# One load for the tiles of two steps in the second phase of a graph-network kernel

## The reference

```python
edge_aggr = jnp.zeros((n, 128)).at[row].add(edge_features)      # 206250 x 128 into 6250 x 128
combined = jnp.concatenate([x, edge_aggr, global_expand], axis=-1) @ W_c + b_c
h = jax.nn.softplus(combined @ W1 + b1)
h = jax.nn.softplus(h @ W2 + b2)
out = _layernorm(x + (h @ W3 + b3), axis=-1)
```

## Time and profile before

| | |
|---|---|
| median of 3 runs | 2045.82 us (2043.21 to 2053.67) |
| the profiled execution's own time | 2045.75 us |
| its span, first to last instruction | 2043.8 us |
| TensorE's granted clock over the span | 0.944 of full |
| busy: TensorE, VectorE, ScalarE, GpSimd | 90%, 64%, 51%, 57% |
| DMA: bytes, mean rate | 413.19 MB, 202 GB/s |
| loads of `members` (L423) | 456 of 258.0 KB, median 3.6 us from issue to landing |

### The profile page before, as it was taken

The page is one execution under the profiler, slowest core; times in us unless marked ns, Lnnn a source line. Parts: engine busy times, 40 slices in busy tenths (PEclk is TensorE's granted clock), DMA queues, the critical chain, the costliest instruction groups (busy, mean ns, idle before and its releaser), DMA issues.

```text
span 2043.8 us, 61008 instructions
## 1 busy us (share of the span) xinstructions
PE 1837.2 (90%) x14853; PEld 1709.6 (84%) x14853; DVE 1309.8 (64%) x3881; ACT 1038.7 (51%) x3479; POOL 1170.9 (57%) x1482
## 2 busy tenths in 40 slices
PE   7888988898898989998998889898988999999986
PEld 4788888888888888887888888788888999999973
DVE  7755555555555555555565555555656998899866
ACT  1443443343444444444443444344446888888886
POOL 1656656656655655665665665565564555555535
PEclk9899988898899999899999898999998999999998
DMA  5488666666656665665565556565657999999942
GB/s 139 156 265 277 198 207 207 202 191 211 207 180 173 174 173 166 175 183 165 172 187 173 172 161 184 163 180 161 186 174 222 299 304 300 296 298 305 304 138 61
DMA packets 166150, 413.19 MB, mean 202 GB/s; under 512 B 28533, under 2 KB 43813, under 8 KB 163896
## 3 DMA queue, kind: packets, MB, share of 16 engines
q1 hardware_dynamic: 103824, 234.69, 38.1%
q0 software_dynamic: 54608, 174.58, 27.5%
q10 hardware_dynamic: 7689, 3.60, 1.0%
HBM read 234.52 MB, written 178.23 MB: 202 GB/s over the span
## 4 chain that ended last, share of the span: by engine, by line
PE 77%; issue 8%; DVE 5%; another core or an unknown queue 3%; POOL 1%; ACT 1%; POOLq 1%; DMA 1%; DVEq 0%; ACTq 0%; SPq 0%
PE ps L1228 51%; PE ps L1300 19%; PE ps L1199 2%; PE ps L1186 2%; DVE arena L803 2%; PE ps L1190 1%; DVE hotc L641 1%; DVE arena L875 1%; PE ps L1335 1%; PE ps L1196 1%; DVE slot_f L660 0%; POOL sums L564 0%; DVE picked L652 0%; POOLq L559 0%
## 5 line engine op out<-in xcount | busy, mean ns | idle before, releaser
L1228 PE MATMUL ps<-arena 128*120 128x129 f32 x9084 | 1229.3, 291 | 98.6 <-issue 87.7
L1228 PEld LDWEIGHTS ps<-arena 128*120 128x120 f32 x9084 | 1141.5, 193 | 130.8 <-issue 117.3
L522 POOL DMA_INDIRECT buckets<-arena,index x757 | 778.8, 1029 | 549.2 <-ACT arena L1013 341.3
L803 DVE TENSOR_SCALAR arena<-slot_no,slot_f 128x360 f32<-128x360 f16 x1514 | 549.1, 415 | 601.3 <-PE ps L1228 332.7
L1013 ACT ACTIVATE arena<-ps 120x387 f32<-120x387 f32 x757 | 372.6, 493 | 851.8 <-PE ps L1228 519.5
L1300 PE MATMUL ps<-mark,members 128*128 128x128 f32 x3648 | 412.7, 276 | 9.0 <-ACT mark L1114 7.1
L1300 PEld LDWEIGHTS ps<-mark,members 128*128 128x128 f32 x3648 | 410.5, 192 | 11.2 <-issue 10.4
L847 DVE TENSOR_SCALAR mark<-node_no,members 128x128 f32<-128x128 f16 x1368 | 360.7, 330 | 55.1 <-DMA members<-buckets 45.9
L564 POOL TENSOR_TENSOR sums<-sums,staged 128x128 f32 x456 | 226.4, 496 | 197.5 <-ACT staged L1102 119.5
L968 ACT ACTIVATE reach<-block_no,arena 128x120 f16<-128x120 f16 x806 | 313.4, 391 | 0.7 <-PE ps L1238 0.7
L1108 ACT ACTIVATE apart<-node_no,members 128x128 f32<-128x128 f16 x456 | 181.0, 397 | 34.3 <-DMA members<-buckets 26.6
(11 more groups left out here) (169 smaller groups left out, 634.6 us busy)
## 6 DMA issues: line engine op xcount, KB each, us to landing
members<-buckets SPq DMA_DIRECT2D x456, 258.0 KB, 3.6
arena<-in_feats SPq DMA_DIRECT2D x201, 516.0 KB
buckets<-arena,index POOLq DMA_INDIRECT x757
xn<-in_x ACTq DMA_DIRECT2D x1, 2800.0 KB
arena<-in_xT SPq DMA_DIRECT2D x11, 250.0 KB, 3.9
out_rows<-xn SPq DMA_DIRECT2D x11, 224.0 KB
buckets<-arena,direct_at POOLq DMA_INDIRECT x98
arena<-in_src SPq DMA_DIRECT2D x1, 805.5 KB
```

Of the source, the lines that this page charges most:

```text
L522: pool.indirect_dma_start(units, bass.IndirectOffsetOnAxis(ap=index[0:SLOTS, s, b:b + 1], axis=0), rows[0:SLOTS, o, :], None).then_inc(sca ...
L803: dve.tensor_scalar(perm[0:TP, b, t, :], slot_no[0:TP, :, :].rearrange("p r b -> p (r b)"), slot_f[0:TP, s, b * TPB + t:b * TPB + t + 1], ...
L1228: mm = pe.matmul(ps[0:SLOTS, MOVED + b, r * ROWF:(r + 1) * ROWF], perm[0:TP, b, t, r * SLOTS:(r + 1) * SLOTS], feat[0:TP, s, b * TPB + t, ...
```

## The change

One load now brings the tiles of two steps, 516 KB, into two neighbouring slots. It is issued when both slots are free, that is, when the later of the two is summed (m + 2 - 8 for m + 1 - 8). It counts one semaphore up for both, so that `members_loaded[m // 2]` stands where `members_loaded[m]` did. In each partition the load has two pieces of 2064 bytes, which lie 258 KB apart in HBM and side by side in SBUF. Lines below the edit stand one lower in the changed kernel.

```diff
--- before.py
+++ after.py
@@ -420,17 +420,18 @@
             sp.wait_ge(filled, 16 * FILLS)
 
             def load_members(s, m):
-                sp.dma_start(members[:, m, :],
-                             buckets[bass.ds(s * TROWS, TROWS), :].rearrange("(p r) f -> p (r f)", r=QR))\
-                  .then_inc(members_loaded[m], 16)
-
-            for m in range(MS):
+
+                sp.dma_start(members[:, m:m + 2, :],
+                             buckets[bass.ds(s * TROWS, 2 * TROWS), :].rearrange("(a p r) f -> p a (r f)", a=2, r=QR))\
+                  .then_inc(members_loaded[m // 2], 16)
+
+            for m in range(0, MS, 2):
                 load_members(m, m)
 
             for c, (t0, nt) in enumerate(chunks):
                 with sp.Fori(1 + c * TURN_X, 1 + (c + 1) * TURN_X if c < NCH - 1 else STEPS // MS) as i:
-                    for m in range(MS):
-                        sp.wait_ge(summed, i * MS + (m + 1 - MS))
+                    for m in range(0, MS, 2):
+                        sp.wait_ge(summed, i * MS + (m + 2 - MS))
                         load_members(i * MS + m, m)
                 sp.dma_start(xt[:, t0 * NP_:(t0 + nt) * NP_], xT[:, t0 * NP_:(t0 + nt) * NP_])\
                   .then_inc(xt_loaded, 16)
@@ -841,7 +842,7 @@
 
 
             def mark_nodes(s, m, turn):
-                dve.wait_ge(members_loaded[m], turn * 16 + 16)
+                dve.wait_ge(members_loaded[m // 2], turn * 16 + 16)
                 wait(dve, summed, s - 3)
                 for r in range(QR - 1):
                     last = dve.tensor_scalar(mark[:, m % 4, r, :], node_no[:, :],
@@ -1103,7 +1104,7 @@
 
 
             def last_apart(s, m, turn):
-                act.wait_ge(members_loaded[m], turn * 16 + 16)
+                act.wait_ge(members_loaded[m // 2], turn * 16 + 16)
                 wait(act, last_marked, s - 1)
                 act.activation(apart[:, m % 2, :], node_no[:, :], ACT.Abs, scale=-1.0,
                                bias=members[:, m, QR * ROWF - 1:QR * ROWF]).then_inc(apart_made, 1)
```

## The result

The changed kernel takes 2133.52 us (median of 4 runs, 2122.50 to 2138.99), the kernel before 2047.76 us (4 runs, 2043.21 to 2053.67): a ratio of 1.0424, with a 95% interval of 1.0392 to 1.0455. The forecast was 2090 us in a range of 2058 to 2125: the direction was right, the loss of 86 us nearly twice the forecast one of 44, and the time lies 8.5 us above the range.

A forecast was written before the change was run, and what follows sets the result against it. TensorE was taken to bound the second phase at 414.6 us, with DMA, VectorE and ScalarE close behind. Pairs at 2.0 us give 456.0, +41.4, plus 0.8 and 2: +44.2 on 2045.75, 2090 us, range 2058 to 2125.

The forecast's parts named there:

- the prediction's ring: Second phase: landing, 0.7 us to step k-1, 1.3 us to next issue, over three pairs; period max(1.80, (L + 2.0) / 3).
- (3): SyncE's issue: the even tile's load goes out one step later, shrinking its room by a step; odd tile unchanged.
- (4): Landing: later for both tiles, since neither counts before 516 KB arrive; 0.8 us for each further tile when the queue is full.
- the room that was left: Second phase before the change: seven steps in the ring, 6.31 us, less 2.0, leave 4.3 us for a load.
- L: Time of a pair's load from issue to landing in the second phase: taken as 4.0 us, between 3.4 and 5.8.
- the sum: Second phase 456.0 us, +41.4; first pair +0.8, xT loads +2; together +44.2 us on 2045.75, giving 2090 us.
- SyncE's halved work: SyncE's loads: half the issues save 0 us, as SyncE waits for TensorE in 370 places.
- The signs that were named: Second phase: landing near 4.0 us, ScalarE's tile waits about 228 and over 100 us, about 456 us, DMA below 0.9, clock 1.00.
- Stays hidden: Rival: pairs land at 3.4 us or sooner, so no change at ScalarE's wait; about 2046 us; chance 0.15.
- the limit of 3.4: Landing in us above which TensorE waits every pair; each 0.1 us of L costs 7.6 us.
- Crowded: Rival: pairs crowd the DMA engines, landing 4.8 us, period 2.27, phase 517 us, 2150 us in all; chance 0.10.
- The third: Rival: waiting every pair lowers TensorE's clock in the second phase, 28 us lost, 2118 us in all; chance 0.08.

The follow-up runs named there:

- run 1: Kernel before with only the issue paired: SyncE waits for the later of two slots, then issues two single 258 KB loads; 1805.66 against 1775.21 us, ratio 1.0171.
- run 2: Kernel before with only the count paired: single loads issued one by one, both tiles wait until both landed; 1795.01 against 1775.21 us, ratio 1.0112.
- run 14: Kernel before with issue and count paired, but two 258 KB loads in a row instead of one of 516 KB; 1839.74 against 1774.30 us, ratio 1.0365.
- run 4: Changed kernel with ScalarE's last_mark(s + 2) put before last_apart(s + 3); 1807.96 us against 1775.21 for the kernel before, ratio 1.0187.
- run 6: Changed kernel with 12 slots for 8, PSUM banks in a ring of six, b3 additions moved; 2076.67 us against 2075.41 for the kernel before, ratio 1.0009.
- run 8: Changed kernel whose loop loads bring only the first half of each piece, 1032 of 2064 bytes; 2072.70 us against 2075.41 for the kernel before, ratio 0.9998.
- run 9: Changed kernel with TensorE's eight passes per step done twice, so that a pair takes 3.6 us; 2472.51 us in one run.
- run 13: The changed kernel unaltered, measured again on one chip beside the two-loads version; 1857.95 us against 1774.30 for the kernel before, ratio 1.0472.
- run 7: Changed kernel with one piece of 4128 bytes per partition instead of two of 2064; 2156.15 us, ratio to the kernel before 1.0384.
- run 5: The changed kernel unaltered, as a yardstick on the other experiments' chip; 2155.46 us against 2075.41 for the kernel before, ratio 1.0388.

## Why the prediction was half right

**The place and the mechanism held.** The loss is in the second phase alone, TensorE waits for tiles, and it does so through ScalarE's look at the first tile of a pair: every stop lies before the odd step, and with ScalarE's order turned before the even one. The table splits the measured periods into the terms of the prediction's ring, (landing + rest) / pairs in the ring. Landings are medians; in run 1 that of the pair's first tile (its row above is for all loads), in run 2 that of its second tile, for which both wait, and in run 14 the time from the first issue to the landing of both. "Rest" is landing to step plus step to issue, the mean over all pairs of the phase:

| kernel | landing | rest | pairs | period by the ring | measured (phase / 228) |
|---|---|---|---|---|---|
| changed kernel | 4.4 | 0.9 + 1.3 | 3 | 2.20 | 500.2 / 228 = 2.19 |
| 1, issue paired | 3.6 | 1.05 + 1.3 | 3 | 1.98 | 452.1 / 228 = 1.98 |
| 2, count paired | 3.4 | 1.05 + 1.3 | 3 | 1.92 | 438.3 / 228 = 1.92 |
| 14, two loads | 4.1 | 0.95 + 1.3 | 3 | 2.12 | 485.6 / 228 = 2.13 |
| 4, mark first | 4.5 | 1.25 + 2.2 | 4 | 1.99 | 451.7 / 228 = 1.98 |
| 6, twelve slots | 4.6 | 2.2, taken over | 5 | 1.36, under TensorE's 1.80 | 413.8 / 228 = 1.81 |

That the sums come out is no proof: the terms are means between the same events, and from one issue to the issue three pairs later they must add up to three periods. The table tells how large each term was. What tests the ring are the periods written down before the runs, with a rest of 2.2 us: 1.93 for run 1 (1.98 measured), 1.93 for run 2 (1.92), 1.91 for run 4 (1.98), and no loss for run 6 (none).

**The later issue and the later landing**, parts (3) and (4) of the prediction, are both real: +30 us (run 1) and +20 us (run 2) alone, +65 us together (run 14). Together they cost more than the two added up, which fits a ring in which each alone first uses up the room that was left (4.3 us for landings of 3.6).

**The term that failed is L, "I take 4.0".** It was chosen between a quiet landing with a further tile (3.0 + 0.8 = 3.8) and the median with one (4.4), nearer the quiet one, on the ground that a phase that waits loads its engines less. It measured 4.4 at the median and 4.35 us in the mean. The further tile was sized well: 2.7 us for 258 KB on a quiet queue (run 8) and 3.6 us for 516 KB (run 9) differ by 0.9. The ground was wrong: with the share of the DMA engines at 0.82 there are still two pairs under way at any time (4.4 us of landing for a period of 2.2), and where only one is, the landing is 0.8 us shorter (run 9). The bytes a second fell from 297 to 245 GB/s, and a pair still met the one before it. (4.35 - 4.0) / 3 x 228 = 27 us of the miss. The median of the whole phase with a tile, 3.6 + 0.8 = 4.4, stood in the text as the nearest row, and I went below it on an argument.

**The rest of the ring was 2.0 and is 2.2.** It was read at one late tile: 0.7 us from landing to step. In the changed kernel it is 0.86 at most pairs that keep TensorE idle, and the step's start to the issue 1.31 in the mean, for 1.3. The late tile of the earlier trace rows was of the short kind: its step started 0.10 us after ScalarE's mark (1707.78 to 1707.88), and in the changed kernel 22 of the 130 stops end so, the other 108 with 0.23 us. Why there are two kinds is not known. The 0.2 us are 0.2 / 3 x 228 = 15 us.

The two terms together are 42 us. The phase was 44.2 us longer than the 456.0 of the sum, and the loss 41.5 us larger than the forecast one (85.8 for 44.2): the sum had 2 us more for the loads beside a piece of `xT`, which the measured landing contains (4.7 us there, 4.3 elsewhere), and what follows the last sum became 2 us shorter. Between 2090 and 2133.52 lie 2 us more, since the sum began with 2045.75 and the kernel before has a median of 2047.76.

**SyncE's halved work was worth nothing**, as said: the instruction takes 0.373 us for two tiles, and SyncE waits 224 times for TensorE. The prediction put the extra time of a longer instruction behind the start of the descriptors. The trace of before does not bear this out: SyncE's first load is issued at 1551.14 and its instruction ends 0.33 us later, but the share of the DMA engines is 0.00 until 1552.0. It changes nothing, since the extra is 0.04 us and is part of the landing as measured.

**The signs that were named.** The waits of ScalarE for tiles passed 100 us (158.5), but there were 193 and not 228, and only 130 pairs stopped TensorE for over 0.3 us from start to start: pairs that land early leave it no gap, and the late ones cost more. The DMA share fell below 0.9 (0.82), the clock was 1.00 behind the first 5.4 us and the last phase was unchanged; the landing was to be near 4.0 us and was 4.4, the phase was to be 456 us and was 500. TensorE's waits are put down to VectorE in the rows, which the prediction would have taken for wrong in kind; the order of the marks and run 4 show that they end at ScalarE.

**The rivals.** "Stays hidden" fell: the least landing of the phase is 3.3 us and the median 1.0 us over the limit of 3.4 (3.2 with the measured rest). "Crowded" was, in its cause, nearer the truth than its chance of 0.10 says: its L was 4.8, and the measured one lies midway between 4.0 and that. (At its period of 2.27 us the engines would be idle a quarter of the time by the prediction's own rate, 0.94 x 1.82 / 2.27 = 0.75, not a fifth.) The third named a clock under 1.00 in the stretch as its proof. It was 0.99, but only by the 0.50 of the first 5.4 us; TensorE's waits behind them took nothing of the clock, so the rival falls. The estimate of 3.2 us for a pair by the Trainium skill, "DMA: Bandwidth & Descriptors", section "Anatomy of one DMA", whose figures are for loads that GpSimd issues, agrees with the traces only for the least landing (3.2 us in run 9); the median with an idle queue is 3.6 and in the ring 4.4 us.

**What stays open.** Why one load of 516 KB lands later than two of 258 KB issued in a row (4.4 against 4.1 us from the first issue, 14 us of the phase, run 13 against 14) is not settled; it is not the number of pieces (run 7) nor SyncE's time for the issue. That the 0.8 us between run 9 and the changed kernel are time spent behind the pair before is read from the two paces, not seen in the trace. And it was not tried to give the pairs ten slots, which would show how little depth is enough.

## What to carry to other kernels

Where a ring of buffers is what binds, its period is (landing + everything from landing back to the next issue) divided by the loads that the ring spans, here three of the four, since a late tile already holds the step before it. Pairing the loads takes room twice, once because the issue waits for the later slot and once because the first tile is not given out until the second is there. Before loads are made larger, count the steps of room that remain and compare them with the landing that the larger load will have at the present rate. In this one case that was the median of the crowded phase plus the further bytes (3.6 + 0.8), not the landing of a quiet one. If the room is short, deepen the ring (12 slots for 8 gave back all of the loss) or let the consumer finish the work for the earlier tile before it waits for the later (gave back 51 of 84 us).

## What the runs showed of the hardware

- A load of 516 KB lands after 3.6 us with a pair every 3.6 us, 4.4 with one every 2.2 us, and 4.6 with one every 1.8 us; 258 KB (in 256 pieces of 1032 bytes) every 1.8 us land after 2.7 us (medians of run 9, the changed kernel, and runs 6 and 8).
- Pieces of 2064 or of 4128 bytes made no difference to the landing of 516 KB (4.3 us in run 5, 4.4 in run 7), though the DMA engines' share was 0.81 with the one and 0.75 with the other.
- After a stop, a step of TensorE starts 0.10 or 0.23 us after the end of the ScalarE instruction that it waited for (22 and 108 of 130 stops in the changed kernel).
- The first phase was some 270 to 300 us shorter on some occasions than on others (first load at 1274 to 1278 against 1543 to 1579 us), at a higher clock (0.984 against about 0.94 over the span; 1.00 against 0.93 from 200 to 1200 us, run 1 and the kernel before), while the changed kernel's second phase and its loads were alike (496 to 500 us, 4.3 to 4.4 us). Whether it is a matter of the chip is not shown: runs recorded for chip 5 have both (runs 1 to 4 the short one, 9 to 12 the long one). The clock is a part of the difference: it stood at its lower level for 61 us in run 1 and for 232 us in the kernel before.
